# Graph network on one core: in the last attention pass, exponentials issued behind tile 9, transposes back behind tile 11, logits ahead of the first one-hot

## The reference

```python
def _gat(x, src, dst, W, a_src, a_dst, b, concat, n):
    H, C = a_src.shape                      # last one: H = 8, C = 64
    h = (x @ W).reshape(n, H, C)
    s_src = (h * a_src).sum(-1)
    s_dst = (h * a_dst).sum(-1)
    e = jax.nn.leaky_relu(s_src[src] + s_dst[dst], NEG_SLOPE)
    m = jax.ops.segment_max(e, dst, num_segments=n)
    ex = jnp.exp(e - m[dst])
    denom = jax.ops.segment_sum(ex, dst, num_segments=n)
    alpha = ex / (denom[dst] + 1e-16)
    out = jax.ops.segment_sum(h[src] * alpha[:, :, None], dst, num_segments=n)
    out = out.reshape(n, H * C) if concat else out.mean(axis=1)
    return out + b
```

## Time and profile before

| | us |
|---|---|
| median of three runs | 10316.04 |
| span of the profiled execution | 10328.9 |
| edge pass of the last attention, from 5594 to 7471 | 1877 |
| busy there: TensorE, GpSimd, VectorE, ScalarE | 1196, 1133, 734, 627 |

### The profile page before, as it was taken

How to read it: one execution, slowest core, us unless ns; L and a number is a source line. 1 busy time by engine, 2 the same in 40 slices (tenths; PEclk the granted TensorE clock), 3 DMA queues, 4 the chain that set the end, 5 groups by cost and what they waited for, 6 DMA issues and landing times. The chain is left out here.

```text
span 10328.9 us, 112817 instructions
## 1 busy us (share of the span) xinstructions
PE 5861.0 (57%) x40667; PEld 5155.4 (50%) x40667; DVE 3843.7 (37%) x8462; ACT 2213.6 (21%) x5853; POOL 5595.9 (54%) x5805
## 2 busy tenths in 40 slices
PE   2444534555366665455554666666569999942232
PEld 1333424444255554344443666666549999932222
DVE  4444523333344443344443334433332222232233
ACT  0000012222033331122221333333311111111111
POOL 7666466666666665666666666666540000036665
PEclk7666656676578876566665788888759999975555
DMA  4555342221133331333322444444318988821111
GB/s 157 174 178 172 79 50 56 54 56 42 48 99 100 99 99 28 93 96 104 100 70 76 120 125 122 124 123 125 81 61 341 353 339 333 334 94 24 23 24 23
DMA packets 445732, 1238.85 MB, mean 120 GB/s; under 512 B 162082, under 2 KB 235683, under 8 KB 401971
## 3 DMA queue, kind: packets, MB, share of 16 engines
q1 hardware_dynamic: 208148, 741.90, 20.6%
q0 software_dynamic: 237024, 489.72, 19.4%
HBM read 1101.15 MB, written 127.51 MB: 119 GB/s over the span
## 5 line engine op out<-in xcount | busy, mean ns | idle before, releaser
L1247 PE MATMUL ps<-pool 128*106 128x128 f32 (+2 forms) x19344 | 3019.8, 319 | 1618.8 <-issue 1018.0
L1247 PEld LDWEIGHTS ps<-pool 128*106 128x106 f32 (+2 forms) x19344 | 2770.2, 195 | 1823.2 <-issue 1202.1
L1205 ACT ACTIVATE ACC<-ps 72x256 f32 (+1 forms) x2418 | 1010.1, 418 | 2530.0 <-remote 1632.8
L470 POOL DMA_INDIRECT ACC<-t,ACC x416 | 392.5, 944 | 1647.2 <-DVE ps L1776 1447.6
L752 POOL DMA_INDIRECT cnt_d<-pool x806 | 832.0, 1032 | 534.2 <-issue 221.5
L1274 POOL DMA_INDIRECT pool<-d_h,srcT_s x806 | 770.8, 956 | 582.1 <-PE ps L1247 296.7
L489 PE MATMUL ps<-pool 128*65 128x128 f32 (+1 forms) x2392 | 468.5, 373 | 1037.8 <-DVE pool L478 600.3
L456 DVE TENSOR_TENSOR ACC<-ACC,ps 65x128 f32 (+1 forms) x1612 | 454.0, 282 | 1443.8 <-remote 1022.6
L1274 POOL DMA_INDIRECT pool<-a_h,srcT_s x806 | 778.3, 966 | 383.1 <-issue 229.8
L1274 POOL DMA_INDIRECT pool<-b_h,srcT_s x806 | 762.7, 946 | 411.6 <-issue 210.2
L1274 POOL DMA_INDIRECT pool<-c_h,srcT_s x806 | 764.1, 948 | 396.9 <-issue 229.3
(11 more groups left out here) (298 smaller groups left out, 5964.3 us busy)
## 6 DMA issues: line engine op xcount, KB each, us to landing
ACC<-cnt_d SPq DMA_DIRECT2D x186, 1600.0 KB, 8.8
pool<-cnt_d SPq DMA_DIRECT2D x94, 1600.0 KB, 8.9
cnt_d<-pool SPq DMA_DIRECT2D x28, 3200.0 KB
ACC<-key_d SPq DMA_DIRECT2D x31, 1664.0 KB
ACC<-key_d SPq DMA_DIRECT2D x25, 2048.0 KB
pool<-seg_d SPq DMA_DIRECT2D x100, 129.0 KB
cnt_d<-pool POOLq DMA_INDIRECT x806
pool<-a_h,srcT_s POOLq DMA_INDIRECT x806
```

The costliest lines, as they stand in the source:

```text
L470: g.indirect_dma_start(out=gb[b][:, k, :], out_offset=None, in_=table, in_offset=bass.IndirectOffsetOnAxis(ap=idx[:, c:c + 1], axis=0)).th ...
L1205: a.activation(win[:, 0:NPL, bass.ds(reg, 128)], pl[0].rearrange("p (i c) -> p i c", c=128), ACT.Copy).then_inc(*(tile_out if last else A) ...
L1247: mm = t.matmul(o, gbr[:, tile % RT, M * i:M * i + M], oh, start=True, stop=True)
```

## The change

The constants of the last attention change, so that the exponentials stand behind tile 9 of a group (not 12) and the transposes back behind tile 11 (not 16). In layer 3 alone the logits of a group are now made ahead of both its one-hots. The other layers keep their constants and their order.

```diff
@@ -931,7 +931,7 @@
             PIECE = 128 // C
-            TURN, BACK, EXP = (7, 15, 11) if C == 64 else (-1, 11, 7)
+            TURN, BACK, EXP = (7, 10, 8) if C == 64 else (-1, 11, 7)
@@ -1153,10 +1153,11 @@
             def vector_edge_prepare(gi):
                 hs = halves(gi)
                 vector_edge_scores(gi)
-                vector_edge_onehot(*hs[0])
+                if layer < 3:
+                    vector_edge_onehot(*hs[0])
                 vector_edge_logits(gi)
-                if len(hs) > 1:
-                    vector_edge_onehot(*hs[1])
+                for half in hs[0 if layer == 3 else 1:]:
+                    vector_edge_onehot(*half)
```

## The result

The changed kernel took 10206.49 us in the median of four runs (10196.19 to 10209.0), the kernel before 10319.39 beside it (10315.06 to 10324.23): ratio 0.9886, 95% interval 0.9872 to 0.990, so 113 us faster where 131 were forecast. The profiled spans are 10207.7 and 10328.9 us.

A forecast was written before the change was run, and what follows sets the result against it. No engine was full; POOL's queue, own work plus waits for TensorE, accounted for the last attention's pass. Saving 2.6 us over 47 groups, 122, plus 9 in the tail gave 131 us: 10185 us, range 10060 to 10300.

The forecast's parts named there:

- The weights' wait: Middle of the last attention's pass: PE's idle for DVE's products, 271.2 us over 47 groups, falls to under 60.
- POOL's queue as the account: Middle groups: POOL's own 28.2 us plus waits fill 35.9 us; 33.3 expected, POOL's waits in the pass 364 to about 240.
- The number of pauses: POOL's queue, middle groups: eight sets in bursts of three leave 2.67 pauses of 1.9 us a group.
- the third burst: POOL's last burst in a group, 5 instructions then 4.70 us idle, can run on, as the next set completes in time.
- The exponential at no cost: ScalarE, behind tile 9: done before PE needs it; cost 0, bounds 0 and 3 us a group, PE's wait under 1.
- The tail: End of the pass, where POOL no longer gathers: two waits for products, 5.3 and 3.94 us, are shed, 9 us.
- Logits ahead of the one-hot at no cost: DVE, layer 3: one-hot moved behind the logits, both done just when weights may start; cost 0, bounds -1.2 to +1.2 us.
- The sum: Last attention's pass: 2.6 us a group times 47 is 122 us, plus 9 at its end, together 131 us.
- The second: Rival for the pass: POOL's work alone bounds, TensorE's lag goes; 9943 us, or 10032 with one pause a group; chance 0.10.
- the rule of the Trainium skill: TensorE never waits on anyone at SBUF, DMAs never contend with compute engines; the trace's 1.8 to 1.9 us lags contradict it.

The follow-up runs named there:

- e2: Kernel before with only the new order in layer 3, logits ahead of the first one-hot; 8991.82 us, ratio 0.9997 to the kernel before.
- e5: The changed kernel unaltered, run again beside the kernel before; 8978.8 us against 8992.64, ratio 0.9986.
- e7: Kernel before, with GpSimd allowed only 24 tiles, not 32, ahead of TensorE's completed tiles in the last attention; 10749.54 us, ratio 1.0414 to the kernel before.
- e8: Changed kernel, with GpSimd allowed only 24 tiles, not 32, ahead of TensorE's completed tiles in the last attention; 10461.19 us, ratio 1.0137 to the kernel before.
- e9: Kernel before, with the last pass's 345 count scatters issued behind the pass; 10485.54 us, ratio 1.0159 to the kernel before.
- e10: Changed kernel, with the last pass's count scatters issued behind the pass; 10163.43 us, ratio 0.9847 to the kernel before.
- e1: Changed kernel with the old order of one-hot and logits, so only transposes back and exponential moved earlier; 8981.57 us against the kernel before's 8994.3, ratio 0.9985.
- e3: Changed kernel with the transposes back still behind tile 16; 8993.11 us, ratio 0.9998 to the kernel before.
- e4: Changed kernel, last attention's gathers replaced by SyncE plain loads, count scatters issued at the start; theory B blamed DMA traffic into memory TensorE reads; 8476.69 us.
- e6: Changed kernel, with GpSimd waiting for the ring every 4 tiles instead of every 2 in the last attention; 8979.38 us, ratio 0.9986 to the kernel before.

## Why the prediction was right

*The weights' wait goes.* Right: 271.2 to 2.8 us in the 47 groups.

*POOL's queue as the account.* Right: forecast 33.3 us a group and about 240 us of POOL's waits, measured 1574 / 47 = 33.5 and 249. That time is POOL's own work plus its waits holds for any version that leaves this work alone; the forecast lay in how many waits would remain. e2 and e5 show that it is the right queue to ask: where POOL hardly waits (14 us) freeing PE of 249 us is worth nothing in the groups. e7 to e10 show the other side: where POOL has less of a lead or less work of its own, the change is worth 288 and 322 us.

*The number of pauses.* Somewhat off: 2.67 a group of 1.9 us forecast. Counted in POOL's queue, gaps over 0.6 us are 140 in the 47 groups, 2.98 a group, 1.75 us in the mean and none over 2.2; before they were 145, with 38 over 3 us. So the third burst did not run on as argued. The change took the long waits down to the length of a pause and left their number; 2.98 x 1.75 = 5.2 us comes out near 2.67 x 1.9 = 5.1 because two errors cancel. That is luck: nearly three pauses of the 1.9 us that were priced would be 5.7 us, 28 us more than forecast over the 47 groups.

*The exponential at no cost.* Mis-sized: PE's wait for it is 67.2 us in 47 groups, 1.4 a group, where under 1 was forecast; single groups show 4.77. How much of it shows in the time is not told apart. The longest one, 15.03 us, stands in the tail behind POOL's last scatters:

```profile
7310.15 0.47 PE L1237 MATMUL ps<-ident,pool 128*128 128x128 f32 x1 [15.03 <-ACT pool L1180]
...
7329.82 12.26 PE L1248 MATMUL ps<-pool 128*106 128x128 f32 x110
```

*The tail.* 9 us forecast, for two waits of 5.3 and 3.94; the last two whole groups took 53.6 and 24.7 us before, 51.3 and 18.2 now, 8.8 less. The number is near, but made up otherwise. The first of the two groups gained 2.3, since in both kernels TensorE stands still there while POOL issues its last scatters (which the prediction overlooked when it wrote that the tail has no POOL cover); the second gained 6.5, the wait of 3.94 and matmuls that now follow without a stop (7329.82).

*Logits ahead of the one-hot at no cost.* No change on a chip that does not lag (e2); not measured alone on one that does.

*The sum.* From its first matmul to its last the pass went from 1833.0 to 1702.1 us, 131 less, the number forecast. That it is the same number is luck: the 47 groups gave 112 where 122 were forecast, and the first group 8 (60.2 to 52.1 us), the last two whole ones 9 and the last six tiles 2, of which the sum had only the 9. The pass starts 4 us later, and the stages after it take 6 us more; the spans differ by 121 and the medians by 113. Why the pass starts later is open. The mean granted clock of the pass rose from 0.80 to 0.83.

*The rivals.* The second (POOL's work alone) describes the chips of e1 to e6: POOL bounds there, but it bounds the kernel before as well, so there is no gain. I had priced it as a gain of 284 to 373 us from a lag that the change itself would take away; the lag was there or not on a given chip, in both kernels. The sentence of the prediction that this case's trace bears the rule of the Trainium skill out badly goes too far; see the last section.

## What to carry to other kernels

When engines wait for each other in a ring, price a freed wait by what it takes from the waits of the queue whose own work nearly fills the time, here GpSimd's; the freed engine's own idle (271 us) is an upper bound that may be worth 113 or 14. Before trusting such a sum, look at whether that queue waits at all, and repeat the comparison on another chip: the same change was worth 1.1% where completions lag and 0.14% where they do not.

## What the runs showed of the hardware

The same program took 8993 to 8998 us on three chips and 10319 to 10323 where the completions of TensorE lag. Each chip was met on one occasion, so the runs do not tell a property of the chip from a state that it was in. The loss is not special to this pass: between the spans of the kernel before and of e2, 1336 us, 806 lie ahead of the pass, 366 in it and 164 behind it.

In e1, e2, e3, e5 and e6 the completion of a set is seen 0.01 us after its last matmul in the median; in the kernel before, on the lagging chip, 5.8 us after in the median for the set of tiles 7 and 8. The lag goes with GpSimd's issuing, not with bytes moved. At the end of the pass before, GpSimd issued scatters (first row, 14 us, DMA share 0.02) and PE got 18 matmuls out; later, with GpSimd silent (second row, 20 us), it got out 162. It did not recover at once: GpSimd's last scatter ended at 7418.4, and ScalarE got its next completion at 7422.3. The third row is a later stage on the same chip: GpSimd is all but silent, 338 GB/s are moved, and each of the 618 completions of TensorE seen in it comes within 0.02 us.

```profile
7404.00:7418.00 14.00, 4.86 (x18) 4.08 (x18) 3.33 (x7) 0.22 (x2) 10.65 (x12) 0.50 0.02 1
7436.00:7456.00 20.00, 20.00 (x162) 19.97 (x161) 7.30 (x12) 10.88 (x29) 0.00 (x0) 0.88 0.00 1
7700.00:9000.00 1300.00, 1270.63 (x13844) 1190.00 (x13845) 328.77 (x909) 189.89 (x453) 1.94 (x2) 0.98 0.89 338
```

So of the theories of e4, the one that blames the bytes (B) has the third row against it even on the lagging chip. On a chip without the lag GpSimd's scatters and 230 GB/s of loads beside TensorE cost it nothing that shows in a group (e4, 19.1 us in both halves). The sentence of the Trainium skill weighed in the prediction ("SBUF — State Buffer", section "Who interferes with whom"), that a DMA never contends with a compute engine, therefore fits both chips as far as the moving of bytes goes. Whether TensorE waits on someone while GpSimd issues, and on what, the traces do not show. What makes the difference between the chips stays open; no run here could tell it.
